# Another order of work at the seams between attentions and MLPs, and a bank of its own for the last inverse sums

## The reference, cut to what matters

```python
x = norm(x + A(x))      # A: LN, 16 heads of 16, window of 128 keys back, w_o, residual; LN, w1 (1024), GELU, w2
y = x
for l in range(2):      # B: 8 heads of 64
    h = shift_token(y)                   # half of the features comes from the token before
    q, k, v = split(h @ wqkv[l]); q, k = rotary(l2norm(q) * qs, l2norm(k) * ks)
    y = y + local_attention(q, k, v) @ wo[l]     # 128 queries see 128 + 128 keys, softmax
    h = LN(shift_token(y)) @ w1[l] + b1[l]
    a, g = split(h)                      # 682 each
    y = y + (a * gelu(g)) @ w2[l] + b2[l]
out = norm(x + y)
```

## Time and profile before

| what | value |
|---|---|
| median of 3 runs (lowest, highest) | 1925.98 us (1923.68, 1926.86) |
| the profiled execution's own time | 1924.92 us |
| its span | 1923.1 us |
| PE, PEld busy | 1830.9 us (95%), 1536.5 us (80%) |
| DVE, ACT, POOL busy | 1572.6 us (82%), 1191.3 us (62%), 1096.9 us (57%) |
| mean granted clock of PE | 0.986 |
| DMA | 116.01 MB, mean 60 GB/s |

### The profile page before, as it was taken

One profiled execution on the slowest core, in us unless ns is written; L12 is line 12 of the kernel. 1 busy time (PEld: TensorE's weight loads), 2 busy tenths in 40 slices (PEclk: granted clock), 3 DMA queues, 4 the chain that ended last, 5 costly groups with the idle time before them and its releaser, 6 DMA issues. The chain is left out here.

```text
span 1923.1 us, 43278 instructions
## 1 busy us (share of the span) xinstructions
PE 1830.9 (95%) x15168; PEld 1536.5 (80%) x15168; DVE 1572.6 (82%) x3853; ACT 1191.3 (62%) x3084; POOL 1096.9 (57%) x1040
## 2 busy tenths in 40 slices
PE   6999999989999899999998999979999999989997
PEld 4777777768998788888887788868888888868886
DVE  6888888867988899999998566779999999957776
ACT  5887777764444677777775333347777777743332
POOL 3565455543444677777674354467777767724443
PEclk9999999999999899999999999989999999989999
DMA  2111111003231211111112333331111111122221
GB/s 99 35 32 32 56 35 34 24 18 117 85 113 33 98 43 47 51 40 49 51 33 64 118 110 113 100 107 33 47 50 38 51 50 39 34 80 66 77 77 33
DMA packets 139667, 116.01 MB, mean 60 GB/s; under 512 B 10440, under 2 KB 138704, under 8 KB 138704
## 3 DMA queue, kind: packets, MB, share of 16 engines
q1 hardware_dynamic: 139472, 113.53, 19.1%
HBM read 75.74 MB, written 37.75 MB: 59 GB/s over the span
## 5 line engine op out<-in xcount | busy, mean ns | idle before, releaser
L1693 ACT ACTIVATE b_probs<-masked,neg_max 128x256 f32<-128x256 f32 (+1 forms) x512 | 250.0, 499 | 3.7 <-DVE neg_max L1238 3.6
L537 PE MATMUL psum<-wa_hi,b_h_hi 128*128 128x512 f32 (+1 forms) x576 | 234.9, 408 | 10.2 <-DVE b_h_lo L1186 9.0
L1238 DVE CUSTOM_DVE_ANT_0 masked<-psum,mask 128x256 f32<-128x256 f32 (+1 forms) x512 | 182.3, 412 | 45.9 <-PE psum L803 35.9
L538 PE MATMUL psum<-wa_lo,b_h_hi 128*128 128x512 f32 (+1 forms) x576 | 215.1, 373 | 0.0
L539 PE MATMUL psum<-wa_hi,b_h_lo 128*128 128x512 f32 (+1 forms) x576 | 215.0, 373 | 0.0
L537 PE MATMUL psum<-g_h_hi,wm_hi 128*128 128x512 f32 (+1 forms) x480 | 191.7, 399 | 7.1 <-POOL g_h_lo L1951 4.6
L538 PE MATMUL psum<-g_h_lo,wm_hi 128*128 128x512 f32 (+1 forms) x480 | 189.8, 395 | 0.0
L539 PE MATMUL psum<-g_h_hi,wm_lo 128*128 128x512 f32 (+1 forms) x480 | 189.7, 395 | 0.0
L1901 POOL TENSOR_TENSOR g_in<-g_in,minus_half 128x16 f32<-128x16 f32 x64 | 188.2, 2941 | 0.7 <-DVE g_in L1198 0.7
L537 PE MATMUL psum<-wm_hi,u_hi 128*128 128x256 f32 x576 | 165.6, 288 | 0.1
L1783 ACT ACTIVATE gate<-psum,vec_b 128x512 f32<-128x512 f32 x96 | 66.0, 687 | 158.0 <-PE psum L539 157.4
(11 more groups left out here) (161 smaller groups left out, 5782.1 us busy)
## 6 DMA issues: line engine op xcount, KB each, us to landing
x_mid<-y_out SPq DMA_DIRECT2D x96, 128.0 KB, 1.7
rope_in<-in_rope SPq DMA_DIRECT2D x64, 128.0 KB, 2.3
x_res<-x_state SPq DMA_DIRECT2D x64, 128.0 KB, 2.2
g_in<-x_mid SPq DMA_DIRECT2D x32, 256.0 KB, 3.8
g_old<-x_state SPq DMA_DIRECT2D x16, 512.0 KB, 4.0
out_x<-g_fin SPq DMA_DIRECT2D x15, 512.0 KB, 3.0
w_raw<-in_w_mlp_b SPq DMA_DIRECT2D x2, 2154.0 KB, 8.9
x_in<-in_x SPq DMA_DIRECT2D x32, 128.0 KB, 2.1
```

The lines of the kernel that those rows point to most:

```text
L537: nc.tensor.matmul(out, a_hi, b_hi, start=first, stop=False)
L538: nc.tensor.matmul(out, a_hi, b_lo, start=False, stop=False)
L1238: ins = nc.vector.tensor_tensor_reduce(out[:, at], src[:, at], (mask if now else mask0)[:, at], -1.0, BIG, ALU.add, ALU.min, neg_max[:, r, ...
L1693: ins = nc.scalar.activation(out, src, ACT.Exp, bias=neg_max[:, r, k:k + 1], scale=-1.0, accum_out=row_sum[:, n % 2, 4 * r + k:4 * r + k + 1])
```

## The change

Nothing is computed otherwise; instructions move within the list of their engine, and one transposition goes to another bank.

Attention A to MLP A. PE: the end of the loop is written out anew, so that values of the last rounds stand ahead of hidden 0 and hidden 1, and out_project of chunk 30, the heads and transposes of chunk 31 stand between the hidden tiles. DVE: statistics one step earlier ((29,2) for (30,2)), normalization too ((30,0) for (31,0)). POOL: the power at (29,2) for (30,3), the low part behind the select of round 126 for behind that of round 125.

Attention B to MLP B. PE: the spread of chunk 31 goes into bank 4, a scores bank, and waits for the last maxima in place of y_out of chunk 30; hidden 1 stands behind out_project of chunk 31 where it stood before it. DVE: in step 31 the statistics stand ahead of the inverse sums and the copy of probabilities, and the normalization ahead of scale_o; in step 32 gain and bias stand ahead of the copy, and the low part in round 1 ahead of scale_o. ACT: g_h_hi ahead of the last copy of probabilities, and in step 31 the exponentials ahead of the copy of the spread sums. POOL: o_low of chunk 28 ahead of the norms of chunk 31, and the power for the MLP ahead of the widening of chunk 30.

MLP to attention B. DVE: h_low of chunk 2 moves from step -1 of the loop into `opening=4`, ahead of the rotation of q of chunk 1.

```diff
+def b_spread(n):
+    return 4 if n == NCH - 1 else 1
...
+                if i > 4 * NCH:
+                    break
...
-                if s == NCH and r > 0:
-                    pe.wait_ge(S["exp_ready"], 4 * NCH)
-                if s == NCH:
-                    pe_mlp(pe, MLP_A, MA, None, opening=r)
+            values(4 * NCH - 2)
+            pe_mlp(pe, MLP_A, MA, None, opening=0)
+            out_project(NCH - 2)
+            values(4 * NCH - 1)
+            pe.wait_ge(S["exp_ready"], 4 * NCH)
+            pe_mlp(pe, MLP_A, MA, None, opening=1)
+            transpose_heads(NCH - 1)
+            pe_mlp(pe, MLP_A, MA, None, opening=2)
+            transpose_o(NCH - 1)
+            pe_mlp(pe, MLP_A, MA, None, opening=3)
+            out_project(NCH - 1)
...
-                if n > 0:
+                if n == NCH - 1:
+                    pe.wait_ge(S["max_ready"], 2 * (g0 + NCH))
+                elif n > 0:
                     pe.wait_ge(S["y_ready"], g0 + n)
+                out = bank[b_spread(n)]
...
                     pe_mlp(pe, MLP_B, MB, layer, opening=0)
+                if (s, r) == (NCH + 1, 0):
                     pe.wait_ge(S["pt_act"], 2 * (g0 + NCH))
                     pe.wait_ge(S["pt_dve"], 2 * (g0 + NCH))
                     pe_mlp(pe, MLP_B, MB, layer, opening=1)
... DVE, attention A
-                if (s, r) == (NCH - 2, 2):
+                if (s, r) == (NCH - 3, 2):
                     dve_mlp(v, MLP_A, MA, None, opening=0)
-                if (s, r) == (NCH - 1, 0):
+                if (s, r) == (NCH - 2, 0):
                     dve_mlp(v, MLP_A, MA, None, opening=1)
... DVE, attention B
             if opening == 4:
+                h_low(2)
                 rotate_q(1)
...
+                    if s == NCH - 1:
+                        dve_mlp(v, MLP_B, MB, layer, opening=0)
                     if b_chunk(s - 1):
                         invert_sums(s - 1)
-                        copy_probs(s - 1, 1)
-                    if s == NCH - 1:
-                        dve_mlp(v, MLP_B, MB, layer, opening=0)
                     if s == NCH:
                         dve_mlp(v, MLP_B, MB, layer, opening=2)
-                        dve_mlp(v, MLP_B, MB, layer, opening=3)
+                    if b_chunk(s - 1):
+                        copy_probs(s - 1, 1)
                 else:
...
+                    if s == NCH - 1:
+                        dve_mlp(v, MLP_B, MB, layer, opening=1)
+                    if s == NCH:
+                        dve_mlp(v, MLP_B, MB, layer, opening=3)
                     if b_chunk(s - 1):
                         scale_o(s - 1)
-                    if s == NCH - 1:
-                        dve_mlp(v, MLP_B, MB, layer, opening=1)
... ACT, attention B
+                    if s == NCH:
+                        act_mlp(a, MLP_B, MB, layer, opening=True)
                     if b_chunk(s - 1):
                         copy_probs(s - 1, 1)
-                    if s == NCH:
-                        act_mlp(a, MLP_B, MB, layer, opening=True)
...
+                    if s == NCH - 1:
+                        exponentials(s, 1)
                     if b_chunk(s - 1):
                         copy_spread(s - 1)
... POOL, attention A
-                if (s, r) == (NCH - 2, 3):
+                if (s, r) == (NCH - 3, 2):
                     pool_mlp(pool, MLP_A, MA, None, opening=0)
-                if (s, r) == (NCH - 1, 3):
+                if (s, r) == (NCH, 0):
                     pool_mlp(pool, MLP_A, MA, None, opening=1)
... POOL, attention B
+                    if s == NCH - 2:
+                        o_low(s - 2)
                     if b_chunk(s + 1) and s + 1 > 1:
                         inverse_norms(s + 1)
-                    if b_chunk(s - 2):
+                    if b_chunk(s - 2) and s != NCH - 2:
                         o_low(s - 2)
+                    if s == NCH - 1:
+                        pool_mlp(pool, MLP_B, MB, layer, opening=0)
                     if b_chunk(s - 1):
                         widen_inverse(s - 1)
-                    if s == NCH - 1:
-                        pool_mlp(pool, MLP_B, MB, layer, opening=0)
```

More of the change, by code:

```diff
@@ L844, in spread_inverse @@
                 pe.wait_ge(S["h_lo"], g0 + min(n + 5, NCH))
-                if n > 0:
+                if n == NCH - 1:
+                    pe.wait_ge(S["max_ready"], 2 * (g0 + NCH))
+                elif n > 0:
                     pe.wait_ge(S["y_ready"], g0 + n)
+                out = bank[b_spread(n)]
                 for t in range(4):
-                    mm = nc.tensor.transpose(W2[:, t * P:t * P + P], b_inv_wide[:, t * P:t * P + P], ident[:])
+                    mm = nc.tensor.transpose(out[:, t * P:t * P + P], b_inv_wide[:, t * P:t * P + P], ident[:])
                 mm.then_inc(S["inv_spread"], 1)
@@ L1294, in dve_attention @@
                         rotate_q(s + 1)
-                    if b_chunk(s + 3) and s + 3 > 1:
+                    if b_chunk(s + 3) and s + 3 > 2:
                         h_low(s + 3)
@@ L1707, in copy_spread @@
                     a.wait_ge(S["o_scaled"], g0 + n)
-                nc.scalar.activation(b_inv_t[:], W2[:], ACT.Copy).then_inc(S["r_copied"], 1)
+                nc.scalar.activation(b_inv_t[:], bank[b_spread(n)][:], ACT.Copy).then_inc(S["r_copied"], 1)
             def o_high(n):
@@ L1756, in act_attention @@
                     if b_chunk(s):
-                        exponentials(s, 1)
+                        if s < NCH - 1:
+                            exponentials(s, 1)
                         copy_probs(s, 0)
```

## The result

| | before | changed |
|---|---|---|
| median (lowest, highest) | 1926.41 us (1923.68, 1926.86), 4 runs | 1906.95 us (1905.08, 1908.15), 4 runs |
| profiled execution, span | 1924.92, 1923.1 us | 1905.08, 1903.4 us |
| PE busy; mean granted clock | 1830.9 us; 0.986 | 1822.6 us; 0.991 |

The ratio is 0.9901, with an interval of [0.9884, 0.9918]. The forecast of 1909 us, with its range of 1902 to 1916, is 2 us off. By the profiles the span is 19.7 us shorter: 8.3 us are busy time of PE that is gone, though PE issues as many instructions as before, and 11.4 us are idle time.

A forecast was written before the change was run, and what follows sets the result against it. PE, busy 95% of the span, was taken as the bound, losing idle time and clock at the seams. Gains of 13.0 + 1.4 + 2.3 = 16.7 us off 1924.92 gave 1908.2, 1909 for the runs; range 1902 to 1916.

The forecast's parts named there:

- Wait of the spread: B to MLP B, step 32: the spread of chunk 31 no longer waits 3.05 us for y_out of chunk 30.
- The lower level behind it: B to MLP B: PE's 5.93 busy us at 1.2 GHz behind that wait return to full clock, 2.97 us won.
- The 0.52 us before hidden 2: B to MLP B: this PE wait goes because hidden 1 now follows out_project of chunk 31; 0.52 us won.
- The step on POOL: Step 30: o_low passes the norms; PE's 2.71 us wait mostly moves to values of chunk 29, 0.3 us won.
- the load of g_in: Step 31: lands at 1696.4, not 1695.3, holding DVE's statistics; just hidden, costing 0.7 if 1 us later.
- The second rival: DVE's queue in step 31 runs later than forecast, 2 us in each seam: 1913 us, chance 0.09.
- ACT's queue in step 31: Four exponentials, 2.0 us, go ahead of the copy of the spread sums; nothing won, nothing lost.
- the third: MLP to B gives the whole wait, as the scores' low parts come earlier too: 1902 us, chance 0.07.
- the fourth: B seams: shorter idle gaps never let the clock rise, so the kernel is slower: 1929 us, chance 0.04.
- The first: B to MLP B: the clock falls anyway in the gap near 1702 to 1705, 2.97 each: 1915 us, chance 0.15.
- The fifth: The spread is free, but the 6.5 us become one wait before hidden 0; other seams cancel: 1925 us, chance 0.03.

The follow-up runs named there:

- the second trace: The changed kernel, unedited, run and profiled once more on another chip: 1905.63 us, ratio 0.9895 to the kernel before there.

## Why the prediction was right

**B to MLP B.** Forecast 6.5 per seam, measured 7.0 and 6.6. Wait of the spread: gone. The lower level behind it: gone in both layers, as forecast; each of these seams still has the one short stretch (1033.9 to 1037.3, 1675.6 to 1679.0) that it had before (1035.0 to 1038.4, 1686.9 to 1690.3). The 0.52 us before hidden 2: gone. PE's idle time fell by 4.2 and 3.8 us in the two seams (3.6 forecast) and the level gave back 2.8 in each (3.0 forecast). That is one execution: the prediction named the level 0.50 between step 31 and hidden 2 as a sign of being wrong, and in the second trace it stands there in the last seam, for 1.7 us. The size of the level's term is thus in part luck. The step on POOL came out as written: PE's 2.71 us for b_o_lo became 2.76 for b_pt.

One step was wrong without harm: that the load of g_in lands 1.1 us later and holds the statistics. Against the chunks ahead of it, y_out of chunk 28 came later by only 0.4 us, and SP issued the last load 2.9 us behind it, 3.9 in the kernel before, so the statistics run directly behind the maxima. DVE after:

```profile
1682.63 0.08 DVE L1257 DVE_READ_ACCUMULATOR2_ANT neg_max<- 128x1 f32 x1
1682.63 1.40 DVE L1384 BATCH_NORM_STATS2 g_stats<-g_in 128x6 f32<-128x256 f32 x4
```

The second rival was therefore off. ACT's queue in step 31 was priced rightly: the exponentials end at 1689.9 and the copy of the spread runs right behind, and values of chunk 31 wait 1.50 us for DVE's copy (1691.11), which stands behind scale_o. That is the wait which the forecast puts in place of the one for g_z; it had given it no size. The wait for g_z fell to 0.47 us, from this in the kernel before:

```profile
1704.20 1.07 PE L939 MATMUL psum<-ident,g_z 128*128 128x128 f32 x8 [1.93 <-DVE g_z L1374]
```

Whose the 3.05 us are was put too simply: "with bank 4 the wait is for maxima" is true, but the bank undone costs 0.8, since y_out too is early once copy, gain and low part are in the new order, and the bank alone leaves 2.37 us of the wait before hidden 0. The forecast's sum is for the whole change, so the size is not touched.

**A to MLP A.** 1.4 forecast, 1.5 measured by the anchors. No run takes this part of the change back, and no median could show so little.

**MLP to B.** The term that was mis-sized: 2.3 us for both, measured 5.4 between the profiles. The wait moved from project_v to the scores as forecast, and the scores begin 1.9 us earlier in each seam beyond what was ahead of them, against 1.6. But what makes up the gain differs between the seams. In the first, PE's idle time fell by only 0.65 us; the rest of the 3.0 is the level, for PE is busy for 8.17 + 3.40 us at 0.50 before and for 6.90 after, and half of the difference is 2.3 us. The forecast had taken it that the level would stay down for as long and only cover other matmuls. In the second, forecast at 0.8, idle time fell by 2.7 us: 4.66 to 3.06 at the wait itself, and the next wait, for ACT's squares, shrank too (before, then after):

```profile
1294.22 1.81 PE L780 MATMUL psum<-ident,g_in 128*128 128x128 f32 x8 [1.85 <-ACT k_sq L1663]
1282.44 1.07 PE L795 MATMUL psum<-ident,g_in 128*128 128x128 f32 x8 [0.57 <-ACT k_sq L1685]
```

There the stretches sum to 13.7 us before and after, with 1.1 us more of busy time in them after, which takes 0.5 us back. The idle time, 3.3 us in both seams together, is the edit's own, since taking the edit back returns 3.4; the other 2 us are the level of these two executions.

**The total.** 16.7 forecast against 19.5 by the medians (and 20.8 on the second chip). By the profiles, 19.7, the surplus of 3.0 is the 3.1 us of MLP to B and 0.7 of the other seams, less the 0.8 by which attention A came later.

Of the rivals, the third and the fourth did not come. The first (the level falls between step 31 and hidden 2) came in one seam of the second trace, at 1.7 us where it was priced at 2.97. The fifth is in kind what the bank alone does. The fourth was priced too low by its own rule: some 20 us of work at full speed take 20 us more at half speed, not 10; nothing else hangs on it. Left open: why the level falls at one place in one execution and at another in the next.

## What to carry to other kernels

A wait that goes is worth what the next late thing leaves of it: 0.7 of 3.05 us for the bank alone, where the MLP's low part took over, about 2 of 5 for the scores, where ACT's squares did. List the whole chain of next waits before you price an edit. When you compare two traces, count PE's idle time and its busy time at the lower level apart: for one program the idle time of a seam repeated to within 0.9 us here, its length only to 2.0. A low clock costs half of PE's busy time only where PE sets the pace; where other engines did, keeping it high gave nothing here.

## What the runs showed of the hardware

The stretches at 1.2 GHz are not tied to the program alone. Within one seam and one program a stretch of 3.4 us is there in one execution and missing in the next, and it costs 1.7 us where PE is busy all through it. And the same work ahead need not have the same outcome: PE was busy for 2.62 of 4.50 us (1687.30 to 1691.80) in one execution and for 2.58 of 4.40 in the other (1684.90 to 1689.30), in both nearly all of it with transposes; the level stayed up behind the one and fell to 0.51 behind the other.
